# Attention scores from full-precision K and Q, four heads at a time, with part of the transposition on VectorE and DMA

## The reference

```python
# x, adj: (32, 256, 256); adj is passed as both matrices of the mask
q, k, v = (proj(Wq, bq), proj(Wk, bk), proj(Wv, bv))        # heads of 32
scores = jnp.einsum('bhqd,bhkd->bhqk', q, k) * SCALE
scores = scores * (adj + adj)[:, None, :, :]
attn = jax.nn.softmax(scores, axis=-1)
ctx = jnp.einsum('bhqk,bhkd->bhqd', attn, v)                 # back to (b, s, 256)
x = _layernorm(x + jnp.einsum('bse,fe->bsf', ctx, Wo) + bo)
```

## Time and profile before

| | |
|---|---|
| median of three runs | 461.89 us |
| the profiled execution | 462.39 us |
| its span | 460.6 us |
| PE busy | 442.1 us (96%) |
| DVE, ACT, POOL busy | 400.5, 384.3, 341.3 us |
| DMA, mean | 223 GB/s, 102.57 MB |
| granted clock of PE, mean | 0.992 |

### The profile page before, as it was taken

How to read it: one execution, slowest core, us unless ns; L and a number is a source line. 1 busy time by engine, 2 the same in 40 slices (tenths; PEclk the granted TensorE clock), 3 DMA queues, 4 the chain that set the end, 5 groups by cost and what they waited for, 6 DMA issues and landing times.

```text
span 460.6 us, 13025 instructions
## 1 busy us (share of the span) xinstructions
PE 442.1 (96%) x3846; PEld 379.3 (82%) x3846; DVE 400.5 (87%) x1713; ACT 384.3 (83%) x1260; POOL 341.3 (74%) x469
## 2 busy tenths in 40 slices
PE   5899999999999999999999999999999999999984
PEld 4587889888888988888898888888888888888763
DVE  4577899988889988988998888899888889989975
ACT  4578898888899888889988888998888899889971
POOL 0454776969788696978869698886969879676555
PEclk9999999999999999999999999999999999999997
DMA  6986555767656576775657676565767656375201
GB/s 228 330 320 265 177 217 182 251 253 282 248 169 263 185 254 253 266 254 174 259 185 261 253 270 241 176 260 186 268 252 264 244 173 261 140 274 207 70 26 68
DMA packets 37335, 102.57 MB, mean 223 GB/s; under 512 B 5905, under 2 KB 14098, under 8 KB 37266
## 3 DMA queue, kind: packets, MB, share of 16 engines
q1 hardware_dynamic: 23762, 75.52, 43.6%
q10 hardware_dynamic: 13504, 26.22, 17.6%
HBM read 26.22 MB, written 8.39 MB: 75 GB/s over the span
## 4 chain that ended last, share of the span: by engine, by line
PE 90%; ACT 4%; POOL 2%; issue 2%; DVE 1%; DMA 1%; POOLq 0%; ACTq 0%; DVEq 0%
PE turn_bank L285 24%; PE proj_bank L313 17%; PE row_bank L273 13%; PE ctx_bank L361 13%; PE out_bank L377 10%; PE out_bank L329 9%; PE inv_bank L344 3%; ACT probs L642 2%; PE row_bank L298 1%; DMA turned_probs<-in_wk 1%; POOL xt_parts L785 1%; PE turn_bank L298 1%; DVE probs L461 0%; ACT whole L673 0%; ACT xt_parts L667 0%
## 5 line engine op out<-in xcount | busy, mean ns | idle before, releaser
L642 ACT ACTIVATE probs<-probs,low_top 128x256 f32<-128x256 f32 x512 | 256.7, 507 | 50.9 <-DVE low_top L469 47.6
L461 DVE CUSTOM_DVE_ANT_0 probs<-row_bank,adj_rows 128x256 f32<-128x256 f32 x512 | 192.1, 413 | 6.5 <-PE row_bank L273 5.9
L476 DVE COPY turned_probs<-turn_bank 128x512 f32<-128x512 f32 x186 | 128.0, 688 | 36.1 <-PE turn_bank L285 36.1
L285 PE MATMUL turn_bank<-ident,probs 128*128 128x128 f32 x1024 | 155.4, 274 | 2.7 <-ACT turned_probs L652 1.9
L285 PEld LDWEIGHTS turn_bank<-ident,probs 128*128 128x128 f32 x1024 | 120.6, 140 | 32.6 <-ACT probs L642 15.5
L273 PE MATMUL row_bank<-stack 128*128 128x256 f32 x512 | 122.9, 322 | 2.3 <-issue 1.9
L313 PE MATMUL proj_bank<-xt_parts,w_parts 128*128 128x512 f32 x360 | 102.8, 395 | 2.0 <-ACT whole L673 1.6
L642 ACT ACTIVATION_READ_ACCUMULATOR probs<-probs,low_top 128x1 f32 x512 | 99.2, 194 | 0.0
L273 PEld LDWEIGHTS row_bank<-stack 128*128 128x128 f32 x512 | 77.1, 191 | 4.7 <-issue 3.6
L779 POOL TENSOR_TENSOR parts<-whole,parts 128x512 fp32r<-128x512 f32 x60 | 77.1, 1284 | 5.0
L800 POOL CAST ctx_parts<-context 128x512 fp32r<-128x512 f32 x31 | 19.0, 611 | 67.2 <-DVE context L489 67.1
(11 more groups left out here) (65 smaller groups left out, 473.1 us busy)
## 6 DMA issues: line engine op xcount, KB each, us to landing
stack<-parts SPq DMA_DIRECT2D x252, 256.0 KB, 3.8
adj_rows<-in_adj ACTq DMA_DIRECT2D x16, 512.0 KB, 4.2
xr<-in_x ACTq DMA_DIRECT2D x16, 512.0 KB, 7.2
out<-result ACTq DMA_DIRECT2D x31, 256.0 KB, 5.0
xt<-in_x_t SPq DMA_DIRECT2D x15, 512.0 KB, 4.7
stack<-parts ACTq DMA_DIRECT2D x4, 256.0 KB, 4.1
xt<-in_x_t SPq DMA_DIRECT2D x2, 256.0 KB, 3.5
turned_probs<-in_wk ACTq DMA_DIRECT2D x1, 256.0 KB, 3.6
```

Source lines behind the costliest of these rows:

```text
L285: last = nc.tensor.transpose(turn_bank[o % 2][:, c * S + t * P:c * S + (t + 1) * P], probs[:, o % RING, t * S + c * P:t * S + (c + 1) * P] ...
L461: last = nc.vector.tensor_tensor_reduce(probs[:, o % RING, t * S:(t + 1) * S], row_bank[o % 2][:, t * S:(t + 1) * S], adj_rows[:, (n // 2) ...
L476: nc.vector.tensor_copy(turned_probs[:, (H * g + o) % TURNED, :], turn_bank[o % 2][:]).then_inc(moved_dve, 1)
L642: last = nc.scalar.activation(tile, tile, ACT.Exp, bias=low_top[:, n % 2, o, t:t + 1], accum_out=sums[:, n % 2, t, o:o + 1])
```

## The change

1. K and Q are no longer cut and stacked. ACT reads each projected chunk into `kq` in whole float32, and the scores are float32 matmuls on a head's own 32 partitions: `rows(n)` makes a **group** of four heads at once, each in its own row quarter of the array and its own bank. All four banks are one set: a group starts when all four heads of the group before have been reduced, and `rows_made` is raised once, behind its last matmul. There are two groups per graph (n = 2g, 2g+1).
2. Three heads of each group (j = 0, 1, 2) are no longer turned by PE. DVE turns their 32 x 32 blocks (`box`, three places after the head's reduction), and SP's queue carries the blocks to their keys' partitions (`carry_boxes`, four DMAs of 192 KB per group). `weigh_v` reads them there, and a copy of V in the same order of keys (`carry_v`, four DMAs of 64 KB per graph). The fourth head is turned by PE as before, into the one `turn_bank` that is left, which also serves the sums' inverse; ACT copies both.
3. The high and low cut of x moves from ACT and POOL to POOL alone. At the start seven small matmuls run ahead of the first projections.
4. The steps are written anew. The core of the diff:

```diff
-            def rows(n, o):
-                wait(pe, rows_used, 8 * n + o - 1)
+            def rows(n):
+                    pe.wait_ge(kq_out, 4 * (pair - 1) + 2 * c + 2)
+                wait(pe, rows_used, J * n)
                 for t in range(T):
-                    last = nc.tensor.matmul(row_bank[o % 2][:, t * S:(t + 1) * S], q[:, t * P:(t + 1) * P], key,
-                                            start=(t == 0), stop=True, skip_group_check=True)
+                    for j in range(J):
+                        own = slice(D * j, D * (j + 1))
+                        last = nc.tensor.matmul(row_bank[j][:, t * S:(t + 1) * S],
+                                                kq[own, pair % 2, 2 * c + 1, b * S + t * P:b * S + (t + 1) * P],
+                                                kq[own, pair % 2, 2 * c, b * S:(b + 1) * S],
+                                                start=(t == 0), stop=True, tile_position=(D * j, 0), skip_group_check=True)
                 last.then_inc(rows_made, 1)
...
+            def turn_probs(n):
+                pe.wait_ge(probs_ready, J * n + J)
+                wait(pe, moved, n)
+                wait(pe, inverted, n // 2)
...
             # project_kq
-                    wait(pe, kq_out, 4 * (pair - 1) + c)
+                    wait(pe, kq_out, 4 * (pair - 1) + k)
...
+            # PE
+            def step(g):
+                ahead = g // 2 + 1
+                if 0 < g < B:
+                    rows(2 * g)
+                if is_pair(ahead):
+                    for half_ in range(2):
+                        project_kq(ahead, 2 * (g % 2), half_)
+                if is_group(2 * g - 1):
+                    turn_probs(2 * g - 1)
+                if is_graph(g + 1):
+                    project_v(g + 1)
+                if is_pair(ahead):
+                    project_kq(ahead, 2 * (g % 2) + 1, 0)
+                if is_graph(g):
+                    rows(2 * g + 1)
+                if is_pair(ahead):
+                    project_kq(ahead, 2 * (g % 2) + 1, 1)
+                if is_graph(g - 1):
+                    turn_shares(g - 1)
+                if 0 <= g - 2 < LAST:
+                    project_out(g - 2)
+                if is_group(2 * g):
+                    turn_probs(2 * g)
+                if is_graph(g - 1):
+                    weigh_v(g - 1)
...
+            # DVE
+            def box(n, j):
+                dve.wait_ge(probs_ready, J * n + j + 1)
+                if j == 0:
+                    wait(dve, carried_in[n % 2], 64 * (n // 2))
+                nc.vector.transpose(boxes[:, n % 2, :, j, :].rearrange("p a (f q) -> p f a q", q=D),
+                                    probs[:, (J * n + j) % RING, :].rearrange("p (f a k) -> p f a k", a=J, k=D)
+                                    ).then_inc(boxed, 1)
...
+                for s in range(H):
+                    n, j = 2 * g + s // J, s % J
+                    if is_group(n):
+                        reduce_rows(n, j)
+                        lower_top(n, j)
+                    behind = H * g + s - LAG
+                    if is_group(behind // J) and behind % J < BOXED:
+                        box(behind // J, behind % J)
+                    if s == 1 and 0 <= g - 2 < LAST:
+                        scale_context(g - 2)
+                    if s == 2 and is_graph(g - 1):
+                        divide(g - 1)
+                    if s == 3 and 0 <= g - 3 < LAST:
+                        for t in range(T):
+                            row_stats(g - 3, t)
+                    if s == 4 and 0 <= g - 3 < LAST:
+                        aggregate(g - 3)
+                    if s == 7 and 0 <= g - 2 < LAST:
                         add_residual(g - 2)
...
+            # ACT
+                    if is_group(n):
+                        exp(n, j)
+                    if s == 2 and is_pair(ahead):
+                        read_kq(ahead, 2 * (g % 2))
+                    if s == 2 and is_group(2 * g - 1):
+                        move_turned(2 * g - 1)
+                    if s == 3 and is_graph(g + 1):
+                        copy_v(g + 1)
+                    if s == 5 and is_graph(g - 1):
                         copy_inverse(g - 1)
+                    if s == 5 and is_pair(ahead):
+                        read_kq(ahead, 2 * (g % 2) + 1)
+                    if s == 7 and is_group(2 * g):
+                        move_turned(2 * g)
...
+            # SP
+                for i in range(J):
+                    sp.dma_start(carried[:, g % 2, c, i].rearrange("p h f -> p (h f)"),
+                                 boxes[D * i:D * (i + 1), n % 2].rearrange("p j h f -> p j (h f)")
+                                 ).then_inc(carried_in[n % 2], 16)
```

More of the change, by code:

```diff
@@ L24 @@
 PAIRS = B // 2
+GROUPS = T * B
 EPS = 1e-5
+WARM = 7
 LOWEST = -3.4028234e38
 FACTOR = 2.0 * float(D) ** -0.5
[L28 to L38, removed]
+RING = 8
+BOXED = J - 1
+LAG = 3
 LAST = B - 1
@@ L135, in wait, with first_bank @@
                 eng.wait_ge(what, value)
[L137 to L156, removed]
+        def first_bank(which, c):
+            return ((proj_bank, ctx_bank), (out_bank, turn_bank))[which][c]
         def weighed(g, half_):
@@ L169, in is_graph, with is_pair, is_group, loads @@
             return 0 <= g < B
[L171 to L181, removed]
[L183 to L206 removed]
+        def is_pair(pair):
+            return 0 <= pair < PAIRS
+        def is_group(n):
+            return 0 <= n < GROUPS
+        def loads(pair):
+            return (pair + 1) // 2
         block = ctx.enter_context(nc.Block())
@@ L354, in weigh_v @@
                     pe.wait_ge(kq_out, 4 * (PAIRS - 1))
-                for o in (H - 1, *ON_ACT[g]):
-                    wait_moved(pe, g, o)
+                pe.wait_ge(moved, 2 * g + 2)
+                for c in range(T):
+                    pe.wait_ge(carried_in[c], 64 * (g + 1))
                 for half_ in range(2):
@@ L404, in make_bias @@
                                             w_whole[:, 3, f, :], start=False, stop=(f == T - 1))
                 last.then_inc(bias_made, 1)
+            pe.wait_ge(ident_ready, 1)
+            for n in range(WARM):
+                nc.tensor.matmul(turn_bank[:, 0:P], ident[:], ident[:], start=True, stop=True, skip_group_check=True)
             project_first(0, [(c, term) for term in TERMS for c in range(T)])
             project_first(1, [(c, term) for c in range(T) for term in TERMS])
+            rows(0)
@@ L707, in _ @@
                 act.sem_inc(stored[n], 16)
-            act.dma_start(w_whole[:, 0], wk).then_inc(weight_in[0], 16)
+            for t in range(T):
+                act.dma_start(w_whole[:, 0, t], wk[:, t]).then_inc(wk_in[t], 16)
             nc.scalar.preload_act_table_set("natural_log_exp_and_others")
             for t in range(T):
-                cut_x(0, t)
+                act.wait_ge(xt_first[t], 16)
+                nc.scalar.copy(xt_parts[:, 0, 0, t, :], xt[:, 0, t, :]).then_inc(first_high, 1)
@@ L758, in step @@
-                    if o == 4 and g - 1 == LAST:
-                        for half_ in range(2):
-                            high_last(half_)
-                    if o == 2 and 0 <= g - 3 < LAST:
-                        store(g - 3)
-            run_steps(step)
+                    if s == 5 and is_pair(ahead):
+                        read_kq(ahead, 2 * (g % 2) + 1)
+                    if s == 7 and is_group(2 * g):
+                        move_turned(2 * g)
+                if g == B:
+                    for half_ in range(2):
+                        high_last(half_)
+                    for n in (B - 3, B - 2):
+                        store(n)
@@ L765, in _ @@
+            for g in range(B + 1):
+                step(g)
             for n in range(2):
```

473 lines of the change are left out of this document (189 added, 284 removed).

## The result

The changed kernel takes 584.16 us (median of 4 runs, 581.02 to 587.44) beside 462.82 for the kernel before in the same session: ratio 1.262, interval 1.257 to 1.267. It is 26% slower. The forecast was 551 in a range of 511 to 600.

The account below looks back on a forecast made before the run. PE, full at 13.47 us a graph, bounded the kernel; afterwards a round through PE, DVE and ACT of 8.2 + 7.7 = 15.9 us would, giving 538 us, plus 13 for the clock: 551, range 511 to 600.

Parts of the forecast that it names:

- DVE's and PE's sums: Work per graph if nobody waits: DVE 13.2 us, PE about 10.3 us, beside PE's 13.47 before.
- the round: One graph's chain through PE, DVE and ACT, halves 8.2 and 7.7 us: 15.9 us against 13.47.
- Both waits: PE's waits for ACT ahead of the second chunk's first half (3.5 us idle) and of turn_probs(2g), scores queued behind.
- The waits overlap where I count them: Rival: DVE's own 13.2 us set the period, 457 us, 1% faster; chance of faster 0.05.
- Scores until DVE starts: First term of each half, from the start of rows to DVE's start: 0.05 + 1.07 + 0.07 = 1.19 us.
- Half a chunk: Three K or Q matmuls on PE behind ACT's read, ahead of rows(2g+1): 0.69 us.
- Turn: Four transposes on PE, turn_probs(2g), behind copy_inverse and ahead of the context product: 0.35 us.
- The clock: PE's idle 3.5 us ahead of rows(2g+1) may lower the clock: 50 us if in all graphs, a quarter counted, 13.
- Start and end: Scores start near 13.8 us; after the last reduction 2.8, 6.2 and 9.9 us follow to the end.
- Both rivals on its rate: DVE's block transpose, taken as 0.61 us: two elements a cycle, 524 us, chance 0.08; two passes, 603 us, 0.07.
- The page beside the sum: Skill page's 3.07 times for four row quarters: 0.26 us more a group, 567 us instead of 551.
- my 0.88: PE's time for a group of 16 score matmuls, 0.88 us, taken from the context product's column quarters.

Follow-up runs that it names:

- e1: Changed kernel with the second chunk's first half of K or Q moved behind rows(2g+1) in PE's program: 522.37 us.
- e2: Changed kernel with rows(2g+2) moved ahead of turn_probs(2g) and the context product in PE's program: 517.28 us.
- e3: Changed kernel with both moves of e1 and e2 in PE's program: 471.19 us, ratio 1.016.
- e6: e3 with DVE's negated maximum moved behind the block transpose of the same place: 457.99 us, ratio 0.991.
- e4: Changed kernel with eleven matmuls of unused result on PE ahead of its wait for ACT's read of K or Q: 564.63 us.
- e8: Changed kernel with all four heads' scores computed from head 0's rows in one row quarter, output not the reference's: 782.48 us (one run).

## Why the prediction held, and where it was off

**The bound and its mechanism: right.** DVE's and PE's sums at 13.2 and 10.3 did not decide; the round did. Both waits stand at the lines named, released as named, and e1 and e2 gave each its price within 0.03 us of what the rows said. "The waits overlap where I count them" (457 us) was wrong for this order and right for the mended one: e3's round at full clock is 13.2, the sum that I gave for DVE, which empties the score banks. Two signs came out less well than named: PE is 76% busy, for 65% to 70%, and the clock column has many 8s. The two probably go together: PE's busy time falls as the clock rises, 439.7 us at 0.89, 395.6 in e3 at 0.952, 383.3 in e6 at 0.981.

**The terms of the round**, from the rows above. Scores until DVE starts: 1.35 and 1.32 for 1.19. DVE and ACT behind them, first half: 291.84 to 298.12, 6.28 for 6.35. Half a chunk: 0.89 for 0.69. Second half: 300.33 to 304.78, 4.45 for 4.26. Turn 0.56 for 0.35, context 1.86 for 1.87. Sum 16.71 for 15.9. **The terms mis-sized** are four. The scores until DVE starts, 0.16 and 0.13: the span was taken from column quarters, 1.07 for the 1.15 measured. Half a chunk and the turn, 0.20 and 0.21. DVE and ACT in the second half, 0.19: the first reduction there takes 0.49 until the next for 0.34, and from the end of ACT's copy (304.63) to PE's start (304.78) 0.15 pass that the sum leaves out. In 31 rounds all this is 20 to 25 us.

Half a chunk and the turn are dearer by what stands around them, not by the wait ahead of them. Without a wait, at full clock, they take 0.89 in e2 (first pair of rows), between the same neighbours, and 0.59 in e3 (second pair), ahead of the same context product:

```profile
278.63 0.96 PE L290 MATMUL proj_bank<-xt_parts,w_parts 128*128 128x512 f32 x3
279.52 1.15 PE L243 MATMUL row_bank<-kq 32*128 32x256 f32 x16
...
259.26 0.66 PE L260 MATMUL turn_bank<-ident,probs 128*128 128x128 f32 x4
259.85 1.27 PE L351 MATMUL ctx_bank<-carried,v_boxed 128*32 128x256 f32 x18
```

I took 0.69 and 0.35 from places with other neighbours: half a chunk between one head's scores and four transposes, and four transposes ahead of one head's scores. The 0.88 that I gave the scores of PE's time is 1.07 now, but PE waits in both halves, and the round doesn't hold this price.

**The clock: right mechanism, half the size.** I counted a quarter of 50 us, 13. By the rows it is 0.7 to 0.9 in each of 31 rounds, 23 to 29 us; e4 gave 0.78 a round back. The clock fell behind nearly every gap, not behind one in four, but a fall cost the scores anything from 0.2 to 0.95 us.

**Start and end.** The first scores start at 11.41 for 13.8. From the last reduction (559.4, the last start of L453) to the end 22.2 us pass for 18.9. The two errors cancel to 1 us, which is luck. 551, 22 for the terms of the round, 13 more for the clock and this 1 make 587, for 583.4 profiled.

**The block transpose: right.** 0.70 own, 0.62 until the next start. Both rivals on its rate fall.

**The page beside the sum.** The Trainium skill, "TensorE: Matmul & The Clock Gate", Part 3, gives 3.07 times for four row quarters at 512 columns. e8 measures 3.4 for these groups of float32 products of 256 columns. The measurement decides: less than four times, as on the page, but not as little. The estimate of a group by the page's figure, 1.14 us, was nearer to the 1.07 measured than my 0.88. What my 0.88 lacks is the ends of a group: it was read between two groups of the same kind, four steps of 0.22, while a group of scores has a first step of 0.32 and a last of 0.30.

## What to carry to other kernels

When a change makes one engine's buffers a single set that two engines hand back and forth, add up the round through all engines before the busy sums: here each engine's sum was at or below the old period, and the round was 3 us above it. Then look at what stands ahead of the hand-over in each in-order program; two groups moved past waits that they did not need gave back 113 of 121 us. An edit that lightens an engine pays only once that engine is the bound, and only down to the next bound: the same DVE edit took 0.8 to 1.0 us a round off DVE's sum both times, and gave 4 us before the moves, in overlapping ranges, and 13 after.

## What the hardware showed unexpectedly

- Two gaps of 3.0 us on PE, a round apart: behind one the granted clock was 0.50, behind the other 1.00. Neither the gap's length nor PE's shorter wait about 10 us ahead of it sorts the 28 such gaps of this trace into the two kinds. What does is open.
- What a PE operation costs until the next start depends on its neighbours. At full clock, in the changed kernel, half a chunk takes 0.80 ahead of transposes and 0.89 ahead of scores in row quarters; four transposes take 0.35 ahead of V's or the output projection and 0.56 ahead of the context product. A wait ahead of them changes this by 0.03 us at most: half a chunk is 0.89 in e2 with and without one, and in e1 four transposes between the output projection and the context product take 0.56 with a wait and 0.53 without.
- Sixteen float32 matmuls in four row quarters take 1.07 us until the next start, in one quarter 3.65. Within the stream the four quarters give the full factor of four, a start every 0.216 us for four matmuls or for one; the two ends of the group, 0.32 and 0.30, stay.
